# A chunk stage in another order, with the angles a chunk sooner, and softplus ended in three vector passes

## What is computed

```python
# text embedding (w, b small; position near 500, so whole turns come off before sine and cosine)
x = x + alpha_age * concat(cos(age * w + b), age * w0 + b0)      # masked for the first 5 tokens
x = x + alpha_abs * concat(sin(position * w + b), position * w0 + b0)
# Mamba, in each of two directions, 384 channels, 16 states
u = silu(conv4(x @ in_w.T))
dt = softplus(dtx @ dt_w.T + dt_b)
h = exp(dt * A) * h + dt * B * u ;  y = sum_n h * C + u * D ;  out = (y * silu(z)) @ out_w.T
```

## Time and profile before

| | |
|---|---|
| time, median of 3 runs | 1898.82 us (1897.49 to 1899.72) |
| profiled execution, its own time | 1895.89 us |
| its span, first to last instruction | 1893.7 us |
| busy share of the span: TensorE, VectorE, ScalarE, GpSimd | 79%, 73%, 46%, 57% |
| mean granted TensorE clock | 0.912 of full speed |
| chunk stage, first scan to the last product | 81.3 to 1408.5 us |
| costliest vector groups | 384 scans of 1756 ns, 384 products of 957 ns |
| costliest GpSimd group | 192 ring products, mean 3473 ns |
| all waits of VectorE's scans for ScalarE's decay | 72.3 us in 46 waits |

### The profile page before, as it was taken

One profiled execution on the slowest core, in us unless ns is written; L12 is line 12 of the kernel. 1 busy time (PEld: TensorE's weight loads), 2 busy tenths in 40 slices (PEclk: granted clock), 3 DMA queues, 4 the chain that ended last, 5 costly groups with the idle time before them and its releaser, 6 DMA issues. The chain is left out here.

```text
span 1893.7 us, 21043 instructions
## 1 busy us (share of the span) xinstructions
PE 1500.1 (79%) x5318; PEld 888.2 (47%) x5319; DVE 1382.1 (73%) x1548; ACT 871.8 (46%) x1946; POOL 1086.9 (57%) x636
## 2 busy tenths in 40 slices
PE   5777877888688678768878777888572799999997
PEld 3433344445344344434444444444242466666665
DVE  4399999998998999899899989998977122222221
ACT  2465545655464565556555545655531122222221
POOL 2376686767758576776676676766740233333333
PEclk8789898998899899889989998999885899999999
DMA  3402122240313124041313312131202634343332
GB/s 86 159 30 105 71 90 83 67 159 19 131 52 110 56 92 150 10 145 37 125 40 108 108 53 101 48 133 58 92 1 83 238 83 91 84 90 88 84 90 51
DMA packets 60428, 165.71 MB, mean 88 GB/s; under 512 B 17086, under 2 KB 29100, under 8 KB 60364
## 3 DMA queue, kind: packets, MB, share of 16 engines
q1 hardware_dynamic: 48220, 148.91, 22.8%
q0 software_dynamic: 12144, 16.13, 4.7%
HBM read 152.98 MB, written 12.03 MB: 87 GB/s over the span
## 5 line engine op out<-in xcount | busy, mean ns | idle before, releaser
L635 POOL TENSOR_TENSOR ring<-dtu,brep 128x1536 f32<-128x1536 f32 x192 | 666.5, 3473 | 377.5 <-DVE states L646 337.7
L658 PE MATMUL py<-ring,ident 128*128 128x384 f32 x1536 | 608.8, 541 | 231.9 <-ACT yg L671 146.1
L646 DVE TENSOR_TENSOR_SCAN states<-states,ring 128x768 f32<-128x768 f32 x384 | 674.2, 1756 | 87.7 <-ACT states L622 72.3
L658 PEld LDWEIGHTS py<-ring,ident 128*128 128x128 f32 x1536 | 303.3, 208 | 507.1 <-issue 156.0
L622 ACT ACTIVATE states<-dt_,aneg 128x376 f32<-128x376 f32 x768 | 405.8, 559 | 0.1
L648 DVE TENSOR_TENSOR ring<-states,crep 128x768 f32<-128x768 f32 x384 | 367.6, 957 | 13.2
L619 ACT ACTIVATE states<-zero_cols 128x16 f32<-128x16 f32 x384 | 70.0, 182 | 514.1 <-DVE ring L648 508.9
L1364 DVE COPY yidx<-place 128x1 int32 (+1 forms) x56 | 8.4, 153 | 246.2 <-DMA out_tokens<-ys,yidx 246.2
L1291 POOL DMA_INDIRECT xs<-x_scratch,yidx x56 | 55.3, 987 | 227.5 <-DVE yweight L1370 149.5
L1318 PE MATMUL gu<-w,xsT 128*128 x440 | 155.2, 496 | 5.5 <-issue 4.9
L467 PE MATMUL pf<-xT,wxz 97*128 97x384 f32 (+1 forms) x384 | 142.5, 509 | 16.1 <-ACT xT L454 8.2
(11 more groups left out here) (228 smaller groups left out, 1561.2 us busy)
## 6 DMA issues: line engine op xcount, KB each, us to landing
brep<-b_c_rows SPq DMA_DIRECT2D x64, 768.0 KB, 3.9
crep<-b_c_rows SPq DMA_DIRECT2D x64, 768.0 KB, 5.9
rest<-in_w_rest SPq DMA_DIRECT2D x55, 384.0 KB, 3.2
w<-in_w SPq DMA_DIRECT2D x8, 768.0 KB, 8.5
wd<-in_wd SPq DMA_DIRECT2D x8, 576.0 KB, 9.3
ptok<-in_p_tok SPq DMA_DIRECT2D x8, 384.0 KB, 3.6
pT<-in_p_T SPq DMA_DIRECT2D x8, 384.0 KB, 4.3
out_tokens<-h SPq DMA_DIRECT2D x8, 288.0 KB, 2.1
```

The costliest lines, as they stand in the source:

```text
L635: gp.tensor_tensor(ring[:, w % NRING], dtu[:, d, o, :].unsqueeze(1).to_broadcast([128, GN, T]), brep[:, ng], ALU.mult).then_inc(dbu_ok, 1)
L646: v.tensor_tensor_scan(h_in, h_in, x_in, 0.0, ALU.mult, ALU.add).then_inc(scan_ok, 1)
L658: mm = pe.matmul(py[:, 0:T], ident[:], ring[:, w % NRING, i, :], start=(ng == 0 and i == 0), stop=False)
```

## The change

1. **softplus.** VectorE's passes w1 = (e + 1) - 1, r = e - w1, dt = dt + r become two: r' = ((1 + e) - 1) - e, where 1 + e comes from ScalarE (`act_plus`, in window 8 or 20, ahead of `z01_out`), and dt = dt - r'. 1 + e is written into `xc`, whose data the convolution has read: rows of 48 out of 54 columns. `x01_out` and `x2_out` must now wait until r' of the direction before is done.
2. **Windows.** `load`, `rows` and `phase` are fetched for chunk c + 2 in windows 14, 16 and 22 of chunk c, instead of for c + 1 in 0, 0 and 1; chunk 0 still does them for chunk 1 in windows 0 and 1. Most steps of DIR go a window later, `x01` and `x01_out` stand in one window, `reduce` goes from 3 to 2, `sin` from 5 to 6, `img` and `embed` to 7, `x1` to 9. The output projection begins at 2, `h2` goes from 7 to 8, `x3` from 10 to 11, ScalarE's part of keep to 8. The gates go a window later, but for the last.
3. **Loop.** `Fori(2, NCH - 2)`; chunk 6 is written out, since it fetches nothing.

```diff
+            else:
+                wait(act, dv.sem, dv.after("r", e - 1))
...
+        def act_plus(act, c, d):
+            e = 2 * c + d
+            act.wait_ge(ds.sem, ds.after("exp1", e))
+            for o in range(1, NC):
+                job_read(act, f"cv{d}_{o}", c)
+            act.activation(one_plus, ea[:].rearrange("p o (b l) -> p (o b) l", l=L), ACT.Identity, bias=1.0).then_inc(ds.sem, 1)
+
+        one_plus = xc[:].rearrange("p o b l -> p (o b) l")[:, :, KC:KC + L]
...
-            v.wait_ge(dv.sem, dv.after("m", e))
-            v.tensor_scalar(dtu[:, d], ea[:], 1.0, -1.0, ALU.add, ALU.add).then_inc(dv.sem, 1)
-            v.wait_ge(dv.sem, dv.after("w1", e))
-            v.tensor_tensor(ea[:], ea[:], dtu[:, d], ALU.subtract).then_inc(dv.sem, 1)
+            v.wait_ge(ds.sem, ds.after("w", e))
+            err = ea[:].rearrange("p o (b l) -> p (o b) l", l=L)
+            v.scalar_tensor_tensor(err, one_plus, -1.0, err, ALU.add, ALU.subtract).then_inc(dv.sem, 1)
             v.wait_ge(dv.sem, dv.after("r", e))
-            v.tensor_tensor(dt_[:, d], dt_[:, d], ea[:], ALU.add).then_inc(dv.sem, 1)
+            v.tensor_tensor(dt_[:, d], dt_[:, d], ea[:], ALU.subtract).then_inc(dv.sem, 1)
...
-        FRONT = {0: ["load", "rows"], 1: ["phase"], 3: ["reduce"], 5: ["sin"], 6: ["img"],
-                 7: ["embed", "embed_rs"], 8: ["x1"], 9: ["xT", "xT_out"]}
-        DIR = {-2: ["x01"], -1: ["x01_out"], 0: ["x2", "conv0", "x2_out", "conv0_out"], 1: ["conv12", "silu"],
-               3: ["bc", "bc_out"], 4: ["bc_store", "dt01", "dt01_out"], 5: ["dt2"], 6: ["dt2_out", "softplus"],
-               7: ["z01", "z01_out"], 8: ["steps", "z2", "z2_out"]}
-        BACK = {3: ["out01"], 4: ["out01_add", "out2"], 5: ["out2_add"], 6: ["rs"], 7: ["h2"],
-                9: ["stat3", "rs3"], 10: ["x3"], 16: ["x3T0"], 18: ["x3T0_out", "x3T1"], 20: ["x3T1_out"],
+        FETCH = {14: ["load"], 16: ["rows"], 22: ["phase"]}
+        FRONT = {2: ["reduce"], 6: ["sin"], 7: ["img", "embed", "embed_rs"], 9: ["x1"], 10: ["xT", "xT_out"]}
+        DIR = {-1: ["x01", "x01_out"], 0: ["x2", "conv0", "x2_out", "conv0_out"], 1: ["conv12"], 2: ["silu"],
+               4: ["bc", "bc_out"], 5: ["bc_store", "dt01", "dt01_out"], 6: ["dt2"], 7: ["dt2_out", "softplus"],
+               8: ["z01", "plus", "z01_out"], 9: ["steps", "z2", "z2_out"]}
+        BACK = {2: ["out01"], 3: ["out01_add"], 4: ["out2"], 5: ["out2_add"], 7: ["rs"], 8: ["h2"],
+                10: ["stat3", "rs3"], 11: ["x3"], 16: ["x3T0"], 18: ["x3T0_out", "x3T1"], 20: ["x3T1_out"],
                 21: ["router"], 23: ["logits"]}
-        KEEP = 6
-        KEPT = 12
+        KEEP = {6: ["keep"], 8: ["keep_x1"], 12: ["kept"]}
         TAKEN = NG
+        GATES = [[TAKEN + 2] * NC, [TAKEN + 2, TAKEN + 2, TAKEN + 1]]
...
-            with eng.Fori(2, NCH - 1) as c:
-                run(eng, steps, plan(c, False, False))
-            run(eng, steps, plan(NCH - 1, False, True))
+            with eng.Fori(2, NCH - 2) as c:
+                run(eng, steps, plan(c, False, False, True))
+            run(eng, steps, plan(NCH - 2, False, False, False))
+            run(eng, steps, plan(NCH - 1, False, True, False))
```

More of the change, by code:

```diff
@@ L213, in build_mamba @@
         fa = Steps(sem("front_act"), "lnp rsp sin lin lnh rsh")
-        dv = Steps(sem("dir_dve"), "m w1 r dt")
-        ds = Steps(sem("dir_act"), "silu x0 exp0 x1 exp1 ln")
+        dv = Steps(sem("dir_dve"), "m r dt")
+        ds = Steps(sem("dir_act"), "silu x0 exp0 x1 exp1 ln w")
         qv = Steps(sem("back_dve"), "stat aggr stat3 aggr3")
@@ L917, in set_up, with plan @@
             eng.wait_ge(w_in, LOADED)
-        FRONT = {0: ["load", "rows"], 1: ["phase"], 3: ["reduce"], 5: ["sin"], 6: ["img"],
-                 7: ["embed", "embed_rs"], 8: ["x1"], 9: ["xT", "xT_out"]}
-        DIR = {-2: ["x01"], -1: ["x01_out"], 0: ["x2", "conv0", "x2_out", "conv0_out"], 1: ["conv12", "silu"],
-               3: ["bc", "bc_out"], 4: ["bc_store", "dt01", "dt01_out"], 5: ["dt2"], 6: ["dt2_out", "softplus"],
-               7: ["z01", "z01_out"], 8: ["steps", "z2", "z2_out"]}
-        BACK = {3: ["out01"], 4: ["out01_add", "out2"], 5: ["out2_add"], 6: ["rs"], 7: ["h2"],
-                9: ["stat3", "rs3"], 10: ["x3"], 16: ["x3T0"], 18: ["x3T0_out", "x3T1"], 20: ["x3T1_out"],
+        FETCH = {14: ["load"], 16: ["rows"], 22: ["phase"]}
[5 more added lines that the diff above has]
+                10: ["stat3", "rs3"], 11: ["x3"], 16: ["x3T0"], 18: ["x3T0_out", "x3T1"], 20: ["x3T1_out"],
                 21: ["router"], 23: ["logits"]}
-        KEEP = 6
-        KEPT = 12
+        KEEP = {6: ["keep"], 8: ["keep_x1"], 12: ["kept"]}
         TAKEN = NG
+        GATES = [[TAKEN + 2] * NC, [TAKEN + 2, TAKEN + 2, TAKEN + 1]]
         SPREAD = {"B": -6, "C": -3}
-        def plan(c, first, last):
+        def plan(c, first, last, fetch):
             slots = [[] for _ in range(U2)]
@@ L958, in plan @@
             taken = [[] for _ in range(U2)]
-            for step, at in (("y_out", TAKEN), ("gate", TAKEN + 1)):
+            for step in ("y_out", "gate"):
                 for d in range(2):
                     for o in range(NC):
-                        w = UD * d + NG * o + at
+                        w = UD * d + NG * o + (TAKEN if step == "y_out" else GATES[d][o])
                         if w < U2:
@@ L969, in plan @@
                 put(BACK, 0, c - 1, 0)
-            slots[KEEP].append(("keep", c, 0))
-            slots[KEPT].append(("kept", c, 0))
+            put(KEEP, 0, c, 0)
+            if first:
+                put({0: FETCH[14] + FETCH[16], 1: FETCH[22]}, 0, 1, 0)
+            if fetch:
+                put(FETCH, 0, c + 2, 0)
             if last:
@@ L997, in in_order @@
             return [(s, c, k) for w in sorted(stage) for s in stage[w]]
-        EARLY = {w: FRONT[w] for w in FRONT if w < 6}
         def early():
-            for step in in_order(EARLY, 0, 0):
-                if step[0] not in ("load", "rows"):
-                    yield step
+            yield "phase", 0, 0
+            yield "reduce", 0, 0
+            yield "sin", 0, 0
         def prologue():
-            yield from (step for step in in_order({w: FRONT[w] for w in FRONT if w not in EARLY}, 0, 0) if step[0] != "img")
+            for step in ("embed", "embed_rs", "x1", "xT", "xT_out"):
+                yield step, 0, 0
             gates = ("z01", "z01_out", "z2", "z2_out")
@@ L1048, in program @@
             run(eng, steps, prologue())
-            run(eng, steps, plan(0, True, False))
-            run(eng, steps, plan(1, False, False))
-            with eng.Fori(2, NCH - 1) as c:
-                run(eng, steps, plan(c, False, False))
-            run(eng, steps, plan(NCH - 1, False, True))
+            run(eng, steps, plan(0, True, False, True))
+            run(eng, steps, plan(1, False, False, True))
+            with eng.Fori(2, NCH - 2) as c:
+                run(eng, steps, plan(c, False, False, True))
+            run(eng, steps, plan(NCH - 2, False, False, False))
+            run(eng, steps, plan(NCH - 1, False, True, False))
             run(eng, steps, epilogue())
@@ L1098, in _ @@
                 "xT_out": lambda e, c, k: act_xT(e, c),
-                "keep": lambda e, c, k: act_keep(e, c),
+                "keep_x1": lambda e, c, k: act_keep(e, c),
                 "x01_out": lambda e, c, d: act_xz(e, c, d, (0, 1)),
@@ L1108, in _ @@
                 "softplus": act_log,
+                "plus": act_plus,
                 "decay": act_decay,
```

## The result

The kernel after the change takes 1842.47 us (median of four runs, 1840.92 to 1843.9) against 1898.15 (1897.14 to 1899.72) for the kernel before, measured beside it: a ratio of 0.9711, 95% interval 0.9697 to 0.9724. The forecast was 1846. Its profiled execution took 1843.9 us, with a span of 1842.1 (before 1895.89 and 1893.7) and a granted clock of 0.911 (0.912).

The account below looks back on a forecast made before the run. VectorE's row of work was taken to bound the kernel. Chunks 1 to 6 gave -43 us, one jump fewer -2.5, chunk 0 -2.3, chunk 7 -4.1, prologue -0.8: -52.7 together, so 1846, range 1820 to 1874.

Parts of the forecast that it names:

- What bounds the kernel: Chunk stage: VectorE's row of work sets the time, busy 1220.6 of 1327.3 us; other engines matter through it.
- Part 1, softplus: Softplus's end on VectorE: four passes become three, saving 0.8 us twice a chunk; ScalarE's plus costs nothing under cover.
- Part 2, silu: ScalarE's silu moved to windows 2 and 14: the 3.16 us wait goes, the 3.43 one shrinks to 2.4.
- Part 3, the other waits: Projections, dt01_out and sin moved: VectorE's waits for ScalarE of 1.84 and 1.07 us go, and 0.4 of small ones.
- Part 4, the reduction: Reduction moved off GpSimd's products: 5.4 us gained a chunk, about 3.0 back through a ring wait and a stand.
- other end: Reduction behind the loop's jump: if the jump costs GpSimd nothing, the stand is 0.4 us instead of 2.95.
- Part 5, the new stand: VectorE's steps in window 9, after h2 moves to 8: passes stand 0.9 and 3.45 us, 4.35 a chunk.
- The sum: Whole kernel: all terms together give -52.7 us, from 1898.8 to 1846.
- Clean passes: Rival: steps and reduction both find GpSimd idle, giving 1798 us, or about 1821 for one alone; chance 0.15.
- Waits that stay: Rival: half of VectorE's waits for ScalarE stay, or the cut-row pass is dearer, about 1873 us; chance 0.17.
- Starvation: Rival: GpSimd's phase in window 22 runs late and delays rings and scan 1, up to 1918 us; chance 0.04.
- No effect: Rival: VectorE's stands grow to what the waits gave, 1899 us; chance 0.04.

Follow-up runs that it names:

- e1: The kernel before with only softplus's end changed to three vector passes, in the old order of windows: 1886.3 us, ratio 0.9943.
- e5: The changed kernel with silu back in the window of its convolution (1 and 13): 1846.31 us, ratio 0.9737.
- e6: The changed kernel with TensorE's dt01 a window sooner, in 4 and 16 instead of 5 and 17: 1839.02 us, ratio 0.9701 to the kernel before.
- e3: The changed kernel with h2 back in window 7 under embed and rs in window 6: 1817.89 us, ratio 0.9586 to the kernel before.
- f3: The changed kernel with GpSimd rounding the whole turns twice, making phase in window 22 3.0 us longer: 1863.37 us, ratio 0.9814.
- e2: The changed kernel's order of windows with the old four softplus passes: 1857.2 us, ratio 0.9788 to the kernel before.
- e7: The changed kernel with chunks 2 to 5 written out, no hardware loop: 1836.42 us, ratio 0.9687 to the kernel before.
- e4: The changed kernel with the reduction in window 3 instead of 2: 1848.49 us, ratio 0.9738 to the kernel before.

## Why the prediction was right, step by step

**What bounds the kernel** held: the gain is VectorE's row of work, 52.3 of it in the stage, and TensorE at 82% of the span sets nothing there but single hand-overs.

**Part 1, softplus.** Right. Counted at 0.8, sixteen times, 12.8; fifteen of them lie in the stage (12.0), where e1 measured 11.6. The cut rows cost 1.35 as taken, `plus` 1.18 (estimate 1.16) and nothing on the path.

**Part 2, silu.** Right on the waits. The one behind window 14 is 2.24 to 2.34 (2.4 predicted), the one behind window 2 is gone in every chunk; in chunk 7, where 2.0 was to stay, the addition of window 3 waits 1.68 for TensorE's output projection instead. But taken as time the part was counted too high: with silu back the stage is only 2.9 longer (e5). The block after the change, chunk 4's ScalarE:

```profile
835.56 1.28 ACT L505 ACT_TABLE_LOAD   x1
836.85 0.52 ACT L509 ACTIVATE u<-ea 128x384 f32<-128x384 f32 x1
...
839.39 1.28 ACT L518 ACT_TABLE_LOAD   x1
840.68 0.19 ACT L629 ACTIVATE states<-zero_cols 128x16 f32<-128x16 f32 x1
```

From 835.56 to 840.68 it is 5.12 us (5.3 counted): the activation after a load starts 0.01 us behind it. The Trainium skill, "ScalarE: Activation LUTs", section "What ACT_TABLE_LOAD costs", adds a drain of about 1380 ns to every switch; this trace has none.

**Part 3, the other waits.** Right where it looked, silent on one place. The wait for `sin` went. That of window 5's projection, which was to go whole, kept 0.98, 0.49, 0.76 and 0.86 at scan 7 of chunks 3 to 5 and 7, 3.1 together; with `dt01` sooner they go (e6). And `dt01` in window 17 also passed behind a sum that waits for y_out, and its lateness cost 8.3 us at scan 19 in seven chunks (e6). The text counted ScalarE's work in that window, and not what the projection itself waits for on TensorE.

**Part 4, the reduction.** Right without a jump: ring wait 1.61 and 1.62 (1.3 predicted) in chunks 1 and 2, 0.92 in chunk 6, stand 1.54 (1.8). With a jump it took the wrong end: 2.95 was taken and 0.15 to 0.3 measured, the "other end" of 0.4. (The sign "first reduction pass 2 to 4 us" failed in these three chunks: it takes 1.1 to 1.3.) GpSimd's jump costs nothing visible, so it runs 2.5 us ahead. Three chunks times 2.7 is 8 us better than counted. Chunk 0, where the phase stays in window 1, became 1.0 us longer instead of 2.3 shorter, but the reduction isn't why: VectorE idles 5.7 us for the turns, the passes take 1.74 and 4.05, and scan 4 comes 1.9 later than before (2.4 counted). The later windows gained 0.9 instead of 4.7: of the missing 3.8 the statistics for chunk 2, which the text sets against chunk 6's, are 1.5, scan 19 is 1.7 and x1 0.7.

**Part 5, the new stand.** Right: 0.9 and 3.45 predicted, 0.45 to 0.54 and 3.23 measured in chunks 1 to 6, 0.12 and 3.23 in chunk 7, and e3 takes it back for 24.6 us. What was missed is the next pass in the row: x1 (L435) takes 1.63 instead of 0.95, since GpSimd's product dt times u (804.87) is now under it, about 0.7 a chunk; that is read from the rows, no run takes it away.

**The sum.** Stage, prologue and rest by the chunks: chunks 1 to 6 -49.2 (predicted -43 and -2.5 for the jump), chunk 0 +1.0 (-2.3), chunk 7 -4.0 (-4.1), prologue -0.7 (-0.8), after the stage +1.3 (0): -51.6 against -52.7. The total is nearer than its terms, and that is luck. The better jump chunks (-8) and the smaller stand (-4, 0.67 in each loop chunk) were paid back by scan 19 (+8.3), scan 7 (+3), x1 (+5) and the slower short passes in the loop; the rest, some 6 us of small gains, is spread over many windows.

**The rivals.** *Clean passes* is now a measured case: with `steps` clean the time is 1817.9 (1821 predicted for one of the two clean). Of the other, half came true: in the three chunks behind a jump the reduction is nearly clean. `steps` isn't, because GpSimd is late by `h2`, and one engine goes while the other stands. *Waits that stay* is excluded: 29.7 us remain, fewer than the 40 set. *Starvation* is excluded at this length of the phase: the second scan waits at most 1.6 us. f3 shows the mechanism is real at the slope given, a microsecond for a microsecond once the slack is used, 1.2 us behind a jump and none elsewhere; it does not test the wait for the router's product, where the text saw 10 us to spare. *No effect* is excluded by the time.

What stays open: Parts 3 and 4 are read from rows, and no run undoes the moves of `reduce`, `sin` or the projections to their old windows. Not shown either is why a short pass in the loop's body hands over later, 0.42 us here and 0.07 in e2 and f3, and why the waits for ScalarE fell by 4.7 us when only the loop went (e7).

## What to carry to other kernels

Before a step moves, ask what it was covering and what covered it: here `h2` lost embed as cover (24.6 us), and the reduction turned out to cover an output projection (e4). Where two engines hold each other up, one long pass that ends half a microsecond late costs a whole pass of the other, so lay such extras in a window in which one of the two has nothing, and look at the windows on both sides. A wait that goes is not yet time that goes: silu's move took away 15.9 us of waits and was worth about 3 (e5). For a moved TensorE step, read what stands ahead of it in TensorE's own order, not only when its inputs are there.

## What the runs showed that was not expected

- A VectorE pass with one SBUF input stands for GpSimd as well, if it is a fast one: 0.76 to 3.88 us for 1152 columns (e2) and 0.95 to 1.63 for the three of x1. The statistics pass, also with one input, doesn't: 1.01 us at 592.35, as elsewhere, with a ring product of GpSimd under it (kernel before, 591.94, 3.47 long). The Trainium skill, "SBUF — State Buffer", section "Who interferes with whom", names tensor_scalar in its fast mode as such a pass, and the trace agrees. It speaks of one engine that blocks the other for an instruction; in the rows read here the held one got its turn next, even with the other's work back to back.
- The hardware loop's jump costs VectorE 2.4 to 2.7 us and GpSimd nothing visible (three ring products in 10.29 us straight through it).
- TensorE, after 4.79 us of idling, had a granted clock of 0.50, the 1.2 GHz level, for 5.5 us, and then 0.94 (windows of chunk 4 of the kernel after; the seventh figure is the clock):

```profile
849.10:854.60 5.50, 5.47 (x9) 2.55 (x9) 5.43 (x5) 2.62 (x7) 4.87 (x4) 0.50 0.29 79
854.60:860.00 5.40, 4.60 (x13) 2.25 (x12) 3.37 (x4) 4.00 (x9) 5.23 (x3) 0.94 0.00 0
```
